# A four-layer graph network on one core: each step of the edge attributes' gathers waits for the one-hots of a histogram step, and gathered rows are stored 32 instead of 8 at a time

## The reference

```python
feat = jnp.concatenate([x[src], edge_weights, x[dst]], axis=1)   # edge_weights = edge_attr_16
h = jax.nn.relu(feat @ W_att1.T + b_att1)
scores = (h @ W_att2.T + b_att2)[:, 0]
m = jax.ops.segment_max(scores, src, num_segments=num_nodes)
e = jnp.exp(scores - m[src])
alpha = e / jax.ops.segment_sum(e, src, num_segments=num_nodes)[src]
msg = jax.ops.segment_sum(alpha[:, None] * lin_x[dst], src, num_segments=num_nodes)
```

## Time and profile before

| | us |
|---|---|
| median of 3 runs | 15592.24 |
| lowest, highest | 15556.44, 15619.84 |
| the profiled execution | 15569.8 |
| its span (first to last instruction) | 15568.0 |

### The profile page before, as it was taken

The page is one execution under the profiler, slowest core; times in us unless marked ns, Lnnn a source line. Parts: engine busy times, 40 slices in busy tenths (PEclk is TensorE's granted clock), DMA queues, the critical chain, the costliest instruction groups (busy, mean ns, idle before and its releaser), DMA issues. The chain is left out here.

```text
span 15568.0 us, 59095 instructions
## 1 busy us (share of the span) xinstructions
PE 2433.1 (16%) x11516; PEld 1918.4 (12%) x11516; DVE 5860.0 (38%) x14807; ACT 2267.7 (15%) x3624; POOL 8805.1 (57%) x8546
## 2 busy tenths in 40 slices
PE   0100000333330000000000001444454431000000
PEld 0000000222220000000000000333343331000000
DVE  8511111988862222222111111455455433222223
ACT  0100000333301111111222210111111100111111
POOL 0477777000007777776777776555555412777776
PEclk7555555555555555555555555777777755555555
DMA  4111110000011111111111111222222201211111
GB/s 147 20 14 13 13 13 13 0 0 0 0 34 42 49 49 49 49 47 49 47 47 47 47 47 39 59 64 60 61 65 61 54 6 13 50 47 49 49 49 46
DMA packets 709731, 627.97 MB, mean 40 GB/s; under 512 B 455664, under 2 KB 538761, under 8 KB 708499
## 3 DMA queue, kind: packets, MB, share of 16 engines
q0 software_dynamic: 273056, 240.52, 8.6%
q1 hardware_dynamic: 434608, 372.85, 7.5%
q10 hardware_dynamic: 1728, 11.11, 0.2%
HBM read 319.01 MB, written 304.83 MB: 40 GB/s over the span
## 5 line engine op out<-in xcount | busy, mean ns | idle before, releaser
L1096 POOL DMA_INDIRECT l_rows<-table,l_sources x4704 | 4936.6, 1049 | 1610.6 <-issue 1576.3
L1096 POOL DMA_INDIRECT l_pair<-table,l_slab x1568 | 1497.0, 955 | 1288.1 <-DMA l_pair<-seeds 794.7
L546 POOL DMA_INDIRECT e_rows<-in_rec,base x1568 | 1690.1, 1078 | 482.9 <-issue 481.6
L982 POOL DMA_INDIRECT seeds<-near_seed,seed_at_d x196 | 189.9, 969 | 2534.3 <-POOLq L910 1909.9
L1293 DVE TENSOR_TENSOR_SCAN l_totals<-l_factor,banks 128x510 f32<-128x510 f32 (+3 forms) x672 | 752.6, 1161 | 1912.1 <-ACT banks L1449 1865.7
L1224 DVE TENSOR_TENSOR l_score<-l_rows,base 128x14 f32<-128x14 f32 x224 | 42.7, 191 | 3210.7 <-DMA l_rows<-table,l_sources 3210.7
L1459 ACT COPY l_kept<-l_totals 128x476 f32<-128x476 f32 (+3 forms) x672 | 638.8, 966 | 3714.6 <-issue 2769.6
L1412 PE MATMUL banks<-ident,l_kept 128*65 128x128 f32 (+2 forms) x4 | 1.9, 464 | 7091.9 <-issue 4653.7
L699 PE MATMUL banks<-Z 125*128 125x98 bf16 x3200 | 623.1, 366 | 3012.6 <-DVE Z L682 2976.8
L407 ACT COPY area<-area 128x2048 f32<-128x2048 f32 x342 | 642.1, 1926 | 2939.1 <-DVE area L332 1688.6
L1402 PE MATMUL banks<-w_each,l_turned 128*128 128x288 f32 (+1 forms) x1344 | 667.4, 586 | 1349.3 <-ACT l_turned L1481 950.5
(11 more groups left out here) (323 smaller groups left out, 5859.1 us busy)
## 6 DMA issues: line engine op xcount, KB each, us to landing
l_rows<-table,l_sources POOLq DMA_INDIRECT x4704
sums<-l_kept SPq DMA_DIRECT2D x112, 476.0 KB
sums<-l_kept SPq DMA_DIRECT2D x224, 231.0 KB
sums<-l_kept SPq DMA_DIRECT2D x112, 462.0 KB
seeds<-zeros SPq DMA_DIRECT2D x130, 392.0 KB
sums<-l_kept SPq DMA_DIRECT2D x112, 448.0 KB
l_pair<-seeds SPq DMA_DIRECT2D x224, 224.0 KB
e_rows<-in_rec,base POOLq DMA_INDIRECT x1568
```

Source lines behind the costliest of these rows:

```text
L546: GP.indirect_dma_start(e_rows[:, u, g, :], None, A["rec16"], bass.IndirectOffsetOnAxis(e_ids[:, s * G16 + g:s * G16 + g + 1], 0)).then_in ...
L1096: GP.indirect_dma_start(pair[:, u, g, 0:D] if gated else rows[:, u, g, :], None, table[l], bass.IndirectOffsetOnAxis(at, 0)).then_inc(rows ...
```

## The change

Two things change in the second block.

1. POOL waits ahead of the 8 gathers of step s until both one-hots of histogram step s are made. The steps by `dst` are numbered 0 to 99 and those by `src` 100 to 199; there are 196 steps of gathers.
2. The ring of 8 steps is kept, but it is filled and emptied in two halves of 4 steps (`E_SAVE`). SP saves a half at once: 49 saves of 288 KB instead of 196 of 72 KB. POOL waits for a half's save ahead of its first step.

```diff
+        E_SAVE = 4
+        ESAVES = ESTEPS // E_SAVE
+        per_half = lambda name, k: [again(f"{name}{h}", k, (ESAVES + 1 - h) // 2) for h in range(2)]
...
-        e_rows_in, e_saved = ring("rows_in", 16 * G16, ESTEPS), ring("saved", 16, ESTEPS)
+        e_rows_in, e_saved = per_half("rows_in", 16 * G16 * E_SAVE), per_half("saved", 16)
...
             def one(s, r, u):
-                if later(s, RING):
-                    pool.wait_ge(*e_saved[u].done(r - 1))
-
+                if u % E_SAVE == 0 and later(s, RING):
+                    pool.wait_ge(*e_saved[u // E_SAVE].done(r - 1))
+
+                pool.wait_ge(*hist["ds"[s // HSTEPS]]["hot"].done(s % HSTEPS))
                 for g in range(G16):
...
-            def save(s, r, u):
-                sp.wait_ge(*e_rows_in[u].done(r))
-                sp.dma_start(to[:, bass.ds(s * G16, G16), :], e_rows[:, u, :, :]).then_inc(e_saved[u].sem, 16)
-
-            in_turn(ESTEPS, RING, [(0, save)])
+            def save(i, r, h):
+                sp.wait_ge(*e_rows_in[h].done(r))
+                n = E_SAVE * G16
+                sp.dma_start(to[:, i * n:(i + 1) * n, :], e_rows[:, E_SAVE * h:E_SAVE * (h + 1), :, :]
+                             ).then_inc(e_saved[h].sem, 16)
+
+            in_turn(ESAVES, 2, [(0, save)])
```

More of the change, by code:

```diff
@@ L530, in build @@
         e_rows = sbt(taking, "e_rows", [P, RING, G16, RE])
-        def ring(name, k, n):
-            return [again(f"{name}{u}", k, n // RING + (u < n % RING)) for u in range(RING)]
+        E_SAVE = 4
+        ESAVES = ESTEPS // E_SAVE
+        per_half = lambda name, k: [again(f"{name}{h}", k, (ESAVES + 1 - h) // 2) for h in range(2)]
         e_ids_in = sem("e_ids_in")
-        e_rows_in, e_saved = ring("rows_in", 16 * G16, ESTEPS), ring("saved", 16, ESTEPS)
+        e_rows_in, e_saved = per_half("rows_in", 16 * G16 * E_SAVE), per_half("saved", 16)
         def take_gpsimd(pool):
@@ L547, in one @@
                                           bass.IndirectOffsetOnAxis(e_ids[:, s * G16 + g:s * G16 + g + 1], 0)
-                                          ).then_inc(e_rows_in[u].sem, 16)
+                                          ).then_inc(e_rows_in[u // E_SAVE].sem, 16)
             in_turn(ESTEPS, RING, [(0, one)])
@@ L555, in take_sync @@
             to = rec_s.rearrange("(p c) w -> p c w", p=P)
-            def save(s, r, u):
-                sp.wait_ge(*e_rows_in[u].done(r))
-                sp.dma_start(to[:, bass.ds(s * G16, G16), :], e_rows[:, u, :, :]).then_inc(e_saved[u].sem, 16)
-            in_turn(ESTEPS, RING, [(0, save)])
-            for u in range(RING):
-                sp.wait_ge(*e_saved[u].done(ESTEPS // RING - 1 + (u < ESTEPS % RING)))
+            def save(i, r, h):
[4 more added lines that the diff above has]
+            in_turn(ESAVES, 2, [(0, save)])
+            for h in range(2):
+                sp.wait_ge(*e_saved[h].done((ESAVES + 1 - h) // 2 - 1))
         nodes0 = ExitStack()
```

## The result

The changed kernel takes 14362.71 us (median of 4 runs, 14317.67 to 14397.72) against 15589.38 for the kernel before (4 runs beside them, 15556.44 to 15619.84): a ratio of 0.9208, 95% interval 0.9189 to 0.9228. The profiled execution took 14370.8 us, its span is 14369.1. The forecast was 14680, with a range of 14300 to 15230.

A forecast was written before the change was run, and what follows sets the result against it. The sort was taken as bound by one-hots waiting for PE's sums, slowed while gathers pile up. From 15569.8 us, 889 came off the sort, with saves and later stages at nothing: 14680 us, range 14300 to 15230.

The forecast's parts named there:

- What bounds the kernel: Sort beside gathers: one-hots wait 1722 us for PE's sum, one PE instruction passing per piled-up gather, 1.4 us each.
- The natural 2015 us: First to last one-hots of the sort: 3737 us less 1722 of waiting, the time DVE needs.
- The coupled pace of 176 intervals: Between one-hots without long work: 12.9 us each, between 13.6 and 12.1, giving a phase of 2848 us, gain 889.
- the pile never forms: Rival: eight gathers are too few to slow PE, POOL paces at 10.8 us per interval; 14310 us, chance 0.14.
- The 23 long intervals, 578 us: Between one-hots, 10 with double COPY_PREDICATEDs and 13 with turns through PE: 578 us, each hiding a gather step whole.
- the favoured 14541 to 14805: Kernel time if the coupled interval is about 12.1 to 13.6 us; chance 0.52.
- The saves at nothing: SP's 49 saves of 288 KB instead of 196 of 72 KB: put at no cost or gain.
- Nothing after the sort: Stages behind the sort: nothing moved, everything as long as before.
- the port lock: Rival: DVE and POOL lock each other out, one-hots wait only for the burst's end; 12.1 us, 14541 us, chance 0.10.
- PE stays slow: Rival: one step's pile takes 24.5 us to drain, 37 us per interval; 18920 us, chance 0.05.
- heavier pile: Rival: the pile grows 0.25 us per gather instead of 0.15, 16 us per interval; 15230 us, chance 0.18.
- stand idle ahead of each step: Sign in the profile afterwards: gathers idle ahead of each step of eight, released by DVE's one-hots L682.

The follow-up runs named there:

- the fillers: Kernel before plus a MEMSET on POOL behind each gather, no wait: 128x400 14506.03 us against 15600.64; 128x100 14072.25 against 15549.49; 128x100 in the first 72 steps only 14950.48.
- the saves alone: The changed kernel without POOL's wait for one-hots, only the larger saves: 12375.0 us against 12393.84 for the kernel before, on a chip without late sums.

## Why the prediction was right, and where it was off

*What bounds the kernel: right.* PE's sum at one instruction per gather, 1.4 us: the period halves with the instructions, and the turns show 11.2 us for eight. That it is the gathers' pace that does it the fillers show. Whether each instruction is bound to one gather, or takes 1.4 us for another reason while a pile stands, no run separates. The natural 2015 us are there wherever no sum is late (2013 with half the matmuls).

*The coupled pace of 176 intervals: wrong in size.* Taken were 12.9 us, between 13.6 and 12.1. Measured: the natural (132 x 10.2 + 44 x 2.06) / 176 = 8.2, and the waits' 302 / 176 = 1.7, so 9.9 us, 176 x 3.0 = 528 us better. Both ends supposed that in each interval eight gathers have to fit, and to be paid for, before the next one-hots. But the wait binds a gather to one-hots, not one-hots to gathers: POOL may lag behind, and it did, catching up in the long intervals (64 stops in 196 steps). And eight gathers make hardly a pile: the first late sum came after forty. The stretched gathers stood in the earlier trace rows, read as a cost to POOL; after 1400 us they are a brake that keeps the pile away. (For the rival "the pile never forms" 27 gathers were counted ahead of the first one-hots; the trace has 24.)

*The 23 long intervals, 578 us: wrong.* They were "long enough to hide a gather step whole". True of the time, not of PE: 13 of them hold the 14 turns, whose transposes fall behind as well if gathers are catching up: 199 us more. In the trace of before the turns are on time (146 us), but there each of them lies behind the last gather; that the change would move them beside gathers was overlooked.

The account with both: 889 + 528 - 199 = 1218, measured 1220. This is no test, since both terms were measured in the same phase. The two errors have opposite signs; the second is the smaller. The measured 14363 lies outside the favoured 14541 to 14805 and only 63 us inside the range's lower end. That end came from the rival "the pile never forms", which had the small pile right and not what sets the pace, so that the range held is in part luck.

*The saves at nothing: right* (0.9205 without them). *Nothing after the sort: right* within 20 us.

*The rivals.* "The pile never forms" gave 14310 and lies nearest, yet its sign (waits near zero) is not there: 302 us of them, and its pace of 10.8 rested on the same eight gathers per interval. Against the port lock stand 22.4 us. "PE stays slow" and "heavier pile" asked how long the pile of one step takes to drain; what has to drain is the pile of 16 to 40 gathers, and it costs 1.7 us per interval in the mean.

*The signs.* L686 ended at 3088, not 3420; "no L682 wait above about 10" (longest 24.4) and "stand idle ahead of each step" were wrong, from the same step. "The sum a few hundred" was right.

## What to carry to other kernels

When an engine waits for a semaphore of PE and PE looks idle, look at what goes out at a steady pace elsewhere and divide the period by PE's instructions: the same quotient at two places (44.8 / 32 and 11.2 / 8) points at the cause, and a run with another count or another pace shows it. Look also at what the change will move beside the stream: a stage that was on time may have been so because it ran alone. A wait that throttles a stream need not fit it into each step; ask how far it may lag, where it catches up, and who else runs there. And before a price is given per interval, ask how many events it takes for the effect to begin at all.

## What the runs showed of the hardware

- On some chips a long stream of indirect gathers at 1.25 us each slows PE step by step to one instruction in 1.4 us, the pace at which gathers are then served; at 1.42 us each no sum and no turn was late. With the filler gone at 1466 us the slow state was back within one turn and stayed until the gathers ended. Where between 1.25 and 1.42 the edge is was not found.
- Other chips show nothing of it with the same kernel and the same pace (12363 to 12394 us against 15549 to 15601). Of the 3195 us between the spans of before and of the saves alone 1722 are the waits of this phase, and 1472 lie behind the sort, 797 of them in layer 2. Which property of a chip decides, and which queue it is that piles up, no run tells.
- A gather beside a TENSOR_TENSOR of DVE mostly takes 1.7 to 2.0 us instead of 0.95 where its shape is 128x1024 (L317, L323); beside L323 of 128x512 it takes 0.95 and beside L317 of 128x512 1.1 to 1.3. Beside COPY_PREDICATED of 128x2048 it is 0.95.
